# Three banks with fixed owners, P pieces by key tile, values of the last heads computed inside the first head, and TensorE transposes for the last rows

## The reference

```python
xn = layernorm(x)                                     # (2048, 256)
k, q, v = W_K xn, W_Q xn, W_V xn                      # 16 heads x 2048 x 128
s = softmax(causal(q k^T) / sqrt(256))                # 16 x 2048 x 2048
out = x + W_O concat(s v) + (fwht(silu(W1 xn) * (W3 xn))) W2
```

## Time and profile before

| | us |
|---|---|
| median of 3 runs | 1433.97 (1431.87 to 1434.05) |
| the profiled execution | 1434.14 |
| its span, first to last instruction | 1432.3 |
| PE / DVE / ACT / POOL busy | 1351.3 / 937.6 / 947.6 / 969.9 |

### The profile page before, as it was taken

One profiled execution on the slowest core, in us unless ns is written; L12 is line 12 of the kernel. 1 busy time (PEld: TensorE's weight loads), 2 busy tenths in 40 slices (PEclk: granted clock), 3 DMA queues, 4 the chain that ended last, 5 costly groups with the idle time before them and its releaser, 6 DMA issues.

```text
span 1432.3 us, 26483 instructions
## 1 busy us (share of the span) xinstructions
PE 1351.3 (94%) x8104; PEld 1192.5 (83%) x8104; DVE 937.6 (65%) x2125; ACT 947.6 (66%) x1918; POOL 969.9 (68%) x640
## 2 busy tenths in 40 slices
PE   5999999889999999999999999999999999999985
PEld 4788888688888888888888888888888888888875
DVE  6533200577777777777777777777777777777760
ACT  4332244477877777878777777777777777777773
POOL 5130000077878787878797979797878787878785
PEclk9999999989999999999999999999999999999997
DMA  4200166588888889888888888898888888888784
GB/s 148 71 0 1 30 192 189 174 259 280 259 278 259 278 259 286 262 285 260 284 278 264 284 262 279 272 287 267 286 253 288 254 278 257 281 262 286 247 268 154
DMA packets 279263, 335.20 MB, mean 234 GB/s; under 512 B 62768, under 2 KB 251312, under 8 KB 274864
## 3 DMA queue, kind: packets, MB, share of 16 engines
q1 hardware_dynamic: 279216, 334.65, 74.4%
HBM read 173.08 MB, written 161.48 MB: 234 GB/s over the span
## 4 chain that ended last, share of the span: by engine, by line
POOL 38%; issue 23%; PE 22%; SPq 7%; DMA 5%; DVE 2%; ACT 2%; POOLq 1%; ACTq 0%; DVEq 0%
POOL pt_lo L401 26%; POOL acc L392 8%; PE ps L882 7%; PE ps L883 7%; PE ps L884 7%; SPq L297 6%; DMA scratch<-raw 4%; POOL v_lo L406 2%; ACT raw L587 1%; POOL wqk_lo L381 1%; DVE raw L824 1%; DMA pt_lo<-scratch 1%; POOL w_raw L359 1%; DVE had L814 1%; DMA acc<-x 1%
## 5 line engine op out<-in xcount | busy, mean ns | idle before, releaser
L401 POOL TENSOR_TENSOR pt_lo<-pt_lo,pt_hi 128x640 fp32r<-128x640 f32 (+11 forms) x384 | 661.6, 1753 | 144.3 <-ACT pt_hi L596 144.3
L587 ACT ACTIVATE raw<-ps,had 128x1024 f32<-128x1024 f32 (+7 forms) x384 | 329.0, 865 | 215.8 <-DVE had L817 201.9
L824 DVE STREAM_TRANSPOSE raw<-raw 128x2048 f32<-128x2048 f32 (+15 forms) x256 | 322.0, 1291 | 98.8 <-ACT raw L587 96.3
L882 PE MATMUL ps<-pt_hi,v_hi 128*128 128x256 f32 (+1 forms) x1152 | 328.4, 285 | 19.4 <-POOL pt_lo L401 13.2
L883 PE MATMUL ps<-pt_lo,v_hi 128*128 128x256 f32 (+1 forms) x1152 | 331.3, 288 | 0.0
L884 PE MATMUL ps<-pt_hi,v_lo 128*128 128x256 f32 (+1 forms) x1152 | 329.8, 286 | 0.0
L596 ACT CAST pt_hi<-pt_lo 128x640 fp32r<-128x640 f32 (+11 forms) x384 | 283.2, 818 | 19.2 <-DMA pt_lo<-scratch 19.2
L814 DVE TENSOR_REDUCE had<-ps 128x1 f32<-128x1024 f32 (+1 forms) x256 | 237.9, 949 | 59.6 <-PE ps L884 59.6
L882 PE MATMUL ps<-k_hi,q_hi 128*128 128x512 f32 (+3 forms) x640 | 239.5, 374 | 13.1 <-ACT raw L587 13.1
L882 PEld LDWEIGHTS ps<-pt_hi,v_hi 128*128 128x128 f32 x1152 | 222.3, 193 | 32.4 <-issue 18.7
L884 PE MATMUL ps<-k_hi,q_lo 128*128 128x512 f32 (+3 forms) x640 | 234.7, 367 | 0.0
(11 more groups left out here) (108 smaller groups left out, 2185.1 us busy)
## 6 DMA issues: line engine op xcount, KB each, us to landing
all_values<-raw SPq DMA_DIRECT2D x16, 1024.0 KB, 5.1
v_next<-all_values SPq DMA_DIRECT2D x16, 1024.0 KB, 5.5
scratch<-raw SPq DMA_DIRECT2D x64, 256.0 KB, 5.5
pt_lo<-scratch SPq DMA_DIRECT2D x16, 1024.0 KB, 5.3
scratch<-raw SPq DMA_DIRECT2D x64, 240.0 KB, 5.0
pt_lo<-scratch SPq DMA_DIRECT2D x16, 960.0 KB, 6.2
scratch<-raw SPq DMA_DIRECT2D x64, 224.0 KB, 5.4
pt_lo<-scratch SPq DMA_DIRECT2D x16, 896.0 KB, 4.7
```

Source lines behind the costliest of these rows:

```text
L401: pool.tensor_tensor(lo, lo.bitcast(F32), hi.bitcast(F32), ALU.subtract).then_inc(pt_lo_done, 1)
L587: act.activation(to[:, first // P:(first + n) // P], ps[:, a * BANK:a * BANK + n].rearrange("p (i g k) -> p i g k", g=4, k=BLK), ACT.Exp, ...
L824: dve.transpose(v, v).then_inc(blocked, 1)
L882: pe.matmul(dst, a[0], b[0], start=start, stop=False, skip_group_check=True)
```

## The change

1. **Banks.** Bank 5 (`BIG`) holds the long z and then the output made from it, bank 7 (`SMALL`) the short z and its output, bank 6 (`KQ`) the projections, except K0, which uses bank 7. A z now waits until the output of the z two before it has been copied (`shared`), not for the split of the z before it. On PE the short z of steps 1, 3, 5 and 7 now stands ahead of the output of the long z, and K2 goes to the end of step 7. On ACT the split of the short z goes in between the pieces of P.
2. **Pieces.** A long row's two pieces of P are cut by key tile, not by query block, and a long z waits for the first piece only, and for the second one at the key tile where it begins.
3. **Late values.** The units of heads 12 to 15 (n = 3) of token tiles 8 to 15 leave the value stage. PE computes two of them in each of steps 0 to 3 of the first head, ACT copies them and SyncE stores them.
4. **End.** The rows of the last head's steps 6 and 7 are not sent to HBM. PE transposes them as 34 tiles of 128 x 128 in ten groups, ACT and DVE split them out of the banks.
5. **Start.** Pairs 4 and 5 are transposed after t = 3 and pairs 6 and 7 after t = 6; ACT's first Hadamard copy and first half weight cast go ahead of its table load; W_V is split during quarter 2. The identity has its own tensor.

The core of the diff:

```diff
+    FIRST_KEYS = {7: (8, 16), 6: (0, 7), 5: (0, 7), 4: (4, 10)}
+
     def key_order(c):
 
-        first = 8 if c in (4, 7) else 0
-        return list(range(first, 2 * c + 2)) + list(range(first))
+        a, b = FIRST_KEYS.get(c, (0, 2 * c + 2))
+        return list(range(a, b)) + list(range(b, 2 * c + 2)) + list(range(a))
+
+    def piece_keys(j, n):
+
+        a, b = FIRST_KEYS.get(j // 2, (0, j + 1))
+        b = min(b, j + 1)
+        return (a, b) if n != 1 else (b, j + 1) if a == 0 else (0, a)
...
+        BIG, KQ, SMALL = 5, 6, 7
...
+        LATE = TILES // 2
+        V_UNITS = [(i, n) for i in range(TILES) for n in range(QUARTERS) if n < 3 or i < LATE]
+        LATE_UNITS = TILES - LATE
+        v_late = w3_raw.rearrange("p k (u m) -> p (k u) m", m=BANK)
+
...
+        def z_bank(z, lo=0, hi=BANK):
+
+            return bank(SMALL if z % 2 else BIG, lo, hi)
+
+        def kq_bank(h, item):
+
+            if isinstance(h, int) and h < 0:
+                return bank(BIG + KQ_ITEMS.index(item) % 3)
+            return bank(SMALL if item == ("K", 0) else KQ)
...
+        def on_tensor(h, s):
+
+            return isinstance(h, int) and h == HEADS - 1 and s >= STEPS - 2
+
+
+        T_LOTS = [[(s, small, i, min(i + 4, row_of(s, small) + 1)) for small in (0, 1)
+                   for i in range(0, row_of(s, small) + 1, 4)] for s in (STEPS - 2, STEPS - 1)]
+        T_GROUPS = T_LOTS[0] + T_LOTS[1]
...
-        PAIRS_AFTER = {1: (2, 3), 2: (4, 5), 3: (6, 7)}
+        PAIRS_AFTER = {1: (2, 3), 3: (4, 5), 6: (6, 7)}
...
+                last = 3 if i < LATE else 2
+                heads = (last + 1) * PER_Q
+                sp.wait_ge(v_copied, v_unit_count(i, last))
+                sp.dma_start(all_values[0:heads, :, i, :].rearrange("h p d -> p h d"),
+                             v_raw[i % 2][:, 0:heads * P].rearrange("p (h d) -> p h d", d=P)
+                             ).then_inc(v_stored[i % 2], 16)
+
+            def store_late(u):
+                sp.wait_ge(late_copied, u + 1)
+                sp.dma_start(all_values[3 * PER_Q:, :, LATE + u, :].rearrange("h p d -> p h d"),
+                             v_late[:, u % 4, :].rearrange("p (h d) -> p h d", d=P)).then_inc(late_stored[u % 4], 16)
 
...
+                    if not on_tensor(h, s):
+                        send(h, s, 0)
+                        send(h, s, 1)
+                    if h == 0 and s < 4:
+                        store_late(2 * s)
+                        store_late(2 * s + 1)
+                    if h == 0 and s == 5:
+                        for i in range(4):
+                            sp.wait_ge(late_stored[i], 16 * LATE_UNITS // 4)
...
+                if not on_tensor(h, s):
+                    to = raw_row(s, small).rearrange("p (g i k) -> p i g k", g=4, k=BLK)
+                    to = to[:, first // P:(first + n) // P]
+                    scores = scores.rearrange("p (i g k) -> p i g k", g=4, k=BLK)
...
+            had_copy(0)
+            gate_weights_to_hi(1, 0)
             act.activation(table_use[:, 1:2], ones[:, :], ACT.Silu)
             for t in range(HT):
                 silu(0, t)
                 if t >= 1:
                     hidden_to_hi(0, t - 1)
-                if t < 2:
-                    had_copy(t)
-                    gate_weights_to_hi(1, t)
...
+                    if c == 2:
+                        wv_to_hi(t)
...
+            def late_copy(u):
+                act.wait_ge(late_projected, u + 1)
+                wait(act, late_stored[u % 4], 16 * (u // 4))
+                act.copy(v_late[:, u % 4, :], bank(SMALL if u % 2 else BIG)).then_inc(late_copied, 1)
 
...
+            def transposed_to_hi(n):
+                s, small, a, b = T_GROUPS[n]
+                act.wait_ge(transposed, n + 1)
+                act.copy(pt_row(pt_hi, row_of(s, small))[:, :, a:b, :], transposed_group(n)).then_inc(t_hi_done, 1)
...
+                    if first and s < 4:
+                        late_copy(2 * s)
+                        late_copy(2 * s + 1)
                     hh, ss = step_before(h, s, 2)
-                    if not (first and s < 2) and not (over and s >= 2):
-                        for n in range(3):
-                            p_to_hi(hh, ss, n)
+                    if over and s < 2:
+                        for n in range(5):
+                            transposed_to_hi(5 * s + n)
+                    if not (first and s < 2) and not over:
+                        p_to_hi(hh, ss, 0)
+                    if s in (1, 3, 5) and not absent(Z_SMALL[s][0]):
+                        z_to_hi(h + Z_SMALL[s][0], Z_SMALL[s][1])
+                    if not (first and s < 2) and not over:
+                        p_to_hi(hh, ss, 1)
+                        p_to_hi(hh, ss, 2)
...
+            def transposed_to_lo(n):
+                s, small, a, b = T_GROUPS[n]
+                j = row_of(s, small)
+                dve.wait_ge(t_hi_done, n + 1)
+                dve.tensor_tensor(pt_row(pt_lo, j)[:, :, a:b, :], transposed_group(n),
+                                  pt_row(pt_hi, j)[:, :, a:b, :].bitcast(F32), ALU.subtract).then_inc(t_lo_done, 1)
...
+                for p in PAIRS_AFTER.get(t, ()):
+                    transpose_xn(p)
                 if t < 2:
                     had_products(t)
-                for p in PAIRS_AFTER.get(t, ()):
-                    transpose_xn(p)
...
+                elif item == ("K", 0):
+                    pe.wait_ge(shared, z_count(h, 1))
+                else:
...
+            def project_late(u):
+                wait(pe, late_copied, u - 1)
+                values_of(bank(SMALL if u % 2 else BIG), LATE + u, 3).then_inc(late_projected, 1)
...
+            def transpose_group(n):
+                s, small, a, b = T_GROUPS[n]
+                if n < 5:
+
+                    pe.wait_ge(exped, piece_count(HEADS - 1, STEPS - 1, exp_of(STEPS - 1, n)))
+                else:
+                    pe.wait_ge(t_lo_done, n - 4)
+                for i in range(a, b):
+                    ins = pe.transpose(bank(n % 5, (i - a) * P, (i - a + 1) * P),
+                                       raw_row(s, small)[:, i * P:(i + 1) * P], ident)
+                ins.then_inc(transposed, 1)
...
-                    wait(pe, z_lo_done, z_count(h, z) - 1)
-                    pe.wait_ge(pt_lo_done, piece_count(h, 2 * (z // 2) + 1, 2 if z % 2 else 1))
+                    wait(pe, shared, z_count(h, z) - 2)
+                    if behind_k:
+                        pe.wait_ge(proj_lo, kq_count(h, ("K", 0)))
+                    if on_tensor(h, 2 * (z // 2)):
+                        pe.wait_ge(t_lo_done, len(T_GROUPS) if z % 2 else 8)
+                    else:
+                        pe.wait_ge(pt_lo_done, piece_count(h, 2 * (z // 2) + 1, 2 if z % 2 else 0))
+                second = 0 if part is None else FIRST_KEYS[c][1] - FIRST_KEYS[c][0]
...
+                    if n and n == second and not on_tensor(h, 2 * (z // 2)):
+
+                        pe.wait_ge(pt_lo_done, piece_count(h, 2 * (z // 2) + 1, 1))
...
+                    if first and s == 4:
+
+                        pe.wait_ge(late_copied, LATE_UNITS)
                     if not absent(Z_BIG[s][0]):
                         weighted_sum(h + Z_BIG[s][0], Z_BIG[s][1], s % 2)
+                    if first and s < 4:
+                        project_late(2 * s)
...
-                        project_kq(h, ("K", 2))
+
+                    if s in Z_SMALL and not absent(Z_SMALL[s][0]):
+                        weighted_sum(h + Z_SMALL[s][0], Z_SMALL[s][1], None, behind_k=s == 7 and more)
                     if s in O_BIG and not absent(O_BIG[s][0]):
                         output(h + O_BIG[s][0], O_BIG[s][1])
-                    if s in Z_SMALL and not absent(Z_SMALL[s][0]):
-                        weighted_sum(h + Z_SMALL[s][0], Z_SMALL[s][1], None)
+                    if s == 7 and more:
+                        project_kq(h, ("K", 2))
 
```

More of the change, by code:

```diff
@@ L855, in period @@
                         z_to_lo(h + O_BIG[s][0], O_BIG[s][1])
-                    if not over:
+                    if over and s < 2:
+                        for n in range(5):
+                            transposed_to_lo(5 * s + n)
+                    if not over and not on_tensor(h, s):
                         transpose_blocks(h, s, 0)
@@ L1072, in period @@
                         project_kq(h, ("K", 0))
+                    if over and s < 2:
+                        for n in range(5):
+                            transpose_group(5 * s + n)
                     if s in O_SMALL and not absent(O_SMALL[s][0]):
```

155 lines of the change are left out of this document (65 added, 90 removed).

## The result

The kernel before takes 1433.06 us (median of 4 runs, 1431.87 to 1434.05), the changed one 1414.42 us (1411.91 to 1417.24): a ratio of 0.9871, 95% interval 0.9848 to 0.9894. That is 19 us faster, against the 44 that I forecast, and outside my range of 1368 to 1407. The profiled execution of the changed kernel took 1413.05 us, span 1411.0.

The account below looks back on a forecast made before the run. PE was taken as the bound, with the send, landing, bring loop right below it. Terms -7.5 - 11.2 - 1.5 - 11.9 - 3 - 9 = -44.1 took 1434.14 us to 1390 us, range 1368 to 1407.

Parts of the forecast that it names:

- Steady heads: Second to fifteenth head: PE's waits shrink, but the free-running send, landing, bring loop limits the gain to -11.9 us.
- nothing in the steady heads: Rival, chance 0.15: in the 14 heads, gaps closed on PE return as waits for DMA; 1402 us.
- The DMA loop gives way: Rival, chance 0.2: in the 14 heads waits for landing shrink, PE loses only V's remainder; 1371 us.
- By PE alone up to 30.7 us would go: 14 heads: all of PE's idle time in the window, 30.7 us, as the far end of the gain.
- The limit of the rate: 14 heads: 272 GB/s against a limit near 358 leaves room, but the send, land, bring order holds the loop.
- The slower rival: Rival, chance 0.05: at head boundaries K2's cast behind late pieces delays the third score bank; 3 us a head gives 1444.
- The late values are not hidden: Rival, chance 0.1: in the first head they delay the scores of steps 0 to 3 one for one; 1403 us.
- Start: Before the value stage: PE's POOL waits ahead of the transposes and the slow stretch behind them go; -7.5 us.
- Values: Value stage: eight units of 1.40 us leave a stage where PE never idles; -11.2 us.
- First head: First head: the eight units are hidden in steps 0 to 3 and part of z's delay comes back; -1.5 us.
- Last head: Last head: the new order cuts PE's 5.4 us idle, with lighter VectorE and SyncE in steps 6 and 7; -3 us.
- end: After the last scores: the HBM round trip for four rows disappears, 34 PE transposes are added; -9 us.

Follow-up runs that it names:

- before_half: The kernel before with half of P's bytes left out of the sends and brings of heads 1 to 15: 1420.81 us, ratio 0.9926.
- v_early: The changed kernel with V's quarters 0 and 1 cast and their remainders taken earlier, z5 added ahead of step 3's pieces: 1410.51 us, ratio 0.9829.
- by_block: The changed kernel with P's pieces cut by query block again, the long z waiting for both pieces: 1411.27 us, ratio 0.9854.
- interleave: The changed kernel with SyncE's order in a step made bring big, send big, bring small, send small: 1393.07 us, ratio 0.9746.
- k2_inter_v: The changed kernel with K2's cast ahead of step 7's pieces, sends and brings interleaved, V's quarters 0 and 1 early: 1382.28 us, ratio 0.9647.
- half_bytes: The changed kernel with half of P's bytes left out of sends and brings in heads 1 to 15, as many DMAs: 1375.66 us, ratio 0.9598.
- late_off: The changed kernel without the late values, all values computed in the value stage again: 1422.3 us, ratio 0.9901.
- k2_first: The changed kernel with ACT's cast of K2 ahead of the three pieces of step 7: 1408.96 us, ratio 0.9833.

## Why the prediction was wrong, step by step

**Steady heads (-11.9, came out +2.5): the step that failed.** I took SyncE's loop as running by itself, and its length as the 992.68 us of the window less the 11.9 that SyncE waited for VectorE and PE. The loop does not run by itself, and the waits for VectorE are not slack on top of it: they grew to 29.3 us where I had them go to nothing. The reading that fits is one ring of exponentials, transposes, sends, landings and pieces, in which a wait that is closed at one place opens at another. What the window holds besides the waits did not shrink either: issuing the sends took SyncE 638.0 us of it before and 641.7 after, and 393.3 with half the bytes. The runs show in its place two bounds close together: the old order of the computing engines at 70.4 us a head (before_half, and no faster by interleaving), and, for the new order, the ring through HBM as SyncE orders it at 71 (71.1 in the changed kernel, 70.8 in v_early, 70.9 in by_block). The change removed the first bound, 1.9 us a head, and met the second at once. What I priced at 70.06 lay at 71. This 71 belongs to the new order of the engines and not to SyncE's queue alone, for the kernel before has the same order of transfers and the same bytes and runs 8 of its 14 heads in 70.4 to 70.5. Which part of the ring the new order made longer stays open; the traces show only that SyncE waits longer for VectorE (29.3 against 7.4 us) and ACT longer for pieces of P (25.4 against 7.7, as I had expected). So "nothing in the steady heads" was the nearest of the rivals: gaps closed on PE came back as waits. Its 1402 us still lies 12 under the measured time, since the other terms came out 8.4 us short together. "The DMA loop gives way" is what interleave and k2_inter_v do, not this change.

**"By PE alone up to 30.7 us would go".** The size was nearly right, by luck: half_bytes lies 28.6 us under the kernel before in the 14 heads (992.7 to 964.0), but only 13.1 of them are idle time of PE (30.7 to 17.6). The other 15.5 are PE's busy time, 961.98 to 946.43 us for the same products, a piece that my sum did not have.

**The limit of the rate.** I set the mean of 272 GB/s against the waits for landing. Windows of 3 us in the changed kernel show what the mean hides:

```profile
390.00:393.00 3.00, 3.00 (x24) 2.83 (x23) 2.69 (x3) 0.81 (x3) 0.11 (x1) 1.00 1.00 347
396.00:399.00 3.00, 1.34 (x3) 1.15 (x4) 2.09 (x3) 1.88 (x5) 3.00 (x3) 0.67 0.48 99
402.00:405.00 3.00, 3.00 (x14) 2.58 (x13) 1.41 (x5) 3.00 (x8) 0.00 (x0) 0.69 1.09 366
```

Full windows move 347 to 366 GB/s, others 99. Laid end to end over the 14 heads, about a quarter of such windows are above 340 and one in eight below 150. What I missed is how close above the old period the order of SyncE binds. (The Trainium skill's page "DMA: Bandwidth & Descriptors", section "Bandwidth", has about 358 GB/s as the limit of a core. These full windows lie around it, others above: 378 GB/s from 281 to 284 us and 389 from 7.5 to 12 us, so the measured rate is not capped there. By the page there was room in the mean, of which interleave's 277 GB/s and k2_inter_v's 279 then took some, and the changed kernel's order none.)

**The slower rival's mechanism was real.** The place, K2's cast behind pieces with a late landing, cost 5.9 us of waits in the trace and a clock at 0.50 for about 7 us. It did not come in each head: 5 waits in 14 heads, the longest 2.7 us. "The late values are not hidden" is excluded by late_off's first head.

**Start (-7.5, came out -3.6).** The waits of 6.6 us on POOL are gone, the first down product stands at 47.93 us, not at 46, and it is W2 that is late:

```profile
PE ps L970 <- DVE pt_lo L824: 2.2, 1, 2.2
```

I had named this chain as the next thing late and its price as the end of the range at -4. The rest is the clock: behind the wait, from 48.8 to 52.4 us, matmuls of 512 columns start 0.43 us apart instead of 0.23, which is 1.5 us given back with the shorter ones; and the first gate, slow in both kernels, is through at 17.71 us instead of 16.57. The mechanism was right and the value taken wrong. The start also differs between traces: the first scores stand between 247.2 and 250.8 us in the runs whose code up to there is the same, so -3.6 is good to some 2 us.

**Values (-11.2):** exact, 78.40 us. **First head (-1.5, +0.8):** 8.6 of 11.2 us hidden, the clock rose only to 0.95, and the wait in front of the first z is 3.9 us where it was 3.63. The profile names no releaser for it; the remainder of P is being made just then, late behind its transfer:

```profile
281.94 2.19 ACT L662 CAST pt_hi<-pt_lo 128x896 fp32r<-128x896 f32 x3 [1.56 <-DMA pt_lo<-scratch]
282.95 5.10 POOL L462 TENSOR_TENSOR pt_lo<-pt_lo,pt_hi 128x896 fp32r<-128x896 f32 x3 [2.49 <-ACT pt_hi L662]
285.13 0.55 PE L970 MATMUL ps<-pt_hi,v_hi 128*128 128x256 f32 x1 [3.92 <-issue]
```

Waiting for one piece instead of two did not help there.

**Last head (-3, -1.9)** and **end (-9, -7.3)** have the right signs; of the end's 11.4 us of waits 4.4 are left:

```profile
PE ps L970 <- DVE z_lo L906: 4.4, 4, 1.9
PE ps L1109 <- DVE pt_lo L913: 0.2, 1, 0.2
```

**My signs.** I had written that a steady head above 71 makes K2's place the thing to look at. It was 71.08, I looked there, and it was mostly the wrong place: k2_first gives 5 us, interleave 21.

## What to carry to other kernels

When transfers stand right above the bound that an edit removes, closing gaps on the busiest engine can only move them, as here: compare the sum of its waits, not their names, and don't price such a loop by taking the issuing queue's waits off its window. Half the bytes, in both kernels, tells in two runs which of two close bounds holds in each; filling a wait with useless work tells whether the clock behind it matters, as long as some of the wait is left behind the fill. The order of sends and brings on one queue was worth some 20 us in one direction and cost 84 in the other.

## What the hardware showed beyond that

How long SyncE needs to issue the same eight DMAs follows their bytes: 3.61 to 5.04 us in half_bytes, 4.76 to 7.38 in the changed kernel. The time of the kernel does not follow the issuing: two DMAs a row took the same time as four with the same bytes (1375.78 against 1375.66 us), though issuing them took 266.3 us of the 14 heads instead of 393.3. A PE wait of 2.33 us for V's remainder (until 512.87) was followed by a window with the clock at 0.52, one of 1.82 (until 654.58) by windows at 1.00:

```profile
513.00:516.00 3.00, 3.00 (x15) 3.00 (x16) 0.00 (x0) 0.95 (x2) 3.00 (x3) 0.52 0.95 275
654.00:657.00 3.00, 2.42 (x20) 2.42 (x21) 0.38 (x3) 1.70 (x4) 3.00 (x3) 1.00 0.67 170
```
